# A routed feed-forward layer on one core: router logits taken from the residual itself, and the normalised rows made on POOL during the search

## The reference

```python
h = _layernorm(x) * (1 + ca) + sa
x = x + ga * attn(h)          # linear attention, then an MLP, each through a layer norm
h = _layernorm(x) * (1 + cb) + sb
x = x + gb * ffn(h)

def ffn(h):                   # E = 8, cap = T // E
    logits = h @ Wg
    probs = softmax(logits, axis=-1)
    top_idx = top_k(probs.T, cap)          # each expert takes its cap best tokens
    tok2exp = the best expert of those that chose the token, else its best expert
    out = gate * (gelu(h @ W1[e]) @ W2[e]) for e = tok2exp
```

## Time and profile before

| | us |
|---|---|
| median of 3 runs | 280.67 |
| the three runs | 280.67, 277.25, 280.97 |
| span of the profiled execution | 278.9 |

### The profile page before, as it was taken

The page is one execution under the profiler, slowest core; times in us unless marked ns, Lnnn a source line. Parts: engine busy times, 40 slices in busy tenths (PEclk is TensorE's granted clock), DMA queues, the critical chain, the costliest instruction groups (busy, mean ns, idle before and its releaser), DMA issues.

```text
span 278.9 us, 4426 instructions
## 1 busy us (share of the span) xinstructions
PE 187.5 (67%) x1151; PEld 145.3 (52%) x1151; DVE 178.5 (64%) x668; ACT 123.8 (44%) x394; POOL 129.5 (46%) x207
## 2 busy tenths in 40 slices
PE   0788989796997788486658989550024995865730
PEld 0545759575776658472524475450014975864620
DVE  2679979999977665989898789600001993532330
ACT  2159964474697765448767443110011441232210
POOL 8737303143555444515991002777750045555652
PEclk9999999999799979757675899976555997999975
DMA  5890000001000000000665000633430324433300
GB/s 157 240 328 30 2 1 0 2 0 39 2 0 1 2 1 0 0 2 25 202 182 158 0 2 5 185 98 109 122 106 19 111 72 145 138 117 99 117 34 28
DMA packets 22009, 20.09 MB, mean 72 GB/s; under 512 B 2464, under 2 KB 19360, under 8 KB 21984
## 3 DMA queue, kind: packets, MB, share of 16 engines
q1 hardware_dynamic: 18752, 14.03, 16.9%
q0 software_dynamic: 2240, 5.51, 6.4%
q10 hardware_dynamic: 992, 0.27, 0.8%
HBM read 13.51 MB, written 6.29 MB: 71 GB/s over the span
## 4 chain that ended last, share of the span: by engine, by line
DVE 36%; PE 29%; another core or an unknown queue 14%; POOL 9%; issue 6%; ACT 4%; POOLq 1%; DVEq 0%
PE pH L940 7%; PE pQ L949 6%; DVE x_sb L1133 6%; DVE scr L1274 5%; DVE bn L988 3%; POOL yr L277 3%; DVE t L1085 2%; POOL rs L277 2%; PE pQ L655 2%; DVE x_sb L1086 2%; DVE rows L996 2%; PE pQ L850 1%; DVE t L1084 1%; DVE mv L991 1%
## 5 line engine op out<-in xcount | busy, mean ns | idle before, releaser
L404 POOL DMA_INDIRECT out_dram<-rows,gidx x28 | 28.4, 1014 | 38.2 <-DVE rows L1422 32.6
L401 POOL DMA_INDIRECT rows<-table_dram,gidx x28 | 27.3, 973 | 32.7 <-DVE gidx L1366 24.5
L940 PE MATMUL pH<-x_sb,hid 128*128 (+1 forms) x140 | 25.2, 309 | 20.3 <-issue 19.8
L949 PE MATMUL pQ<-ew,u 128*128 (+1 forms) x140 | 24.7, 303 | 18.6 <-DVE dig L1446 8.8
L621 ACT ACTIVATE u<-pH 128x256 f32<-128x256 f32 x35 | 13.3, 385 | 45.4 <-PE pH L940 30.1
L940 PEld LDWEIGHTS pH<-x_sb,hid 128*128 128x128 f32 x140 | 21.0, 215 | 21.8 <-issue 21.7
L949 PEld LDWEIGHTS pQ<-ew,u 128*128 128x128 f32 x140 | 20.3, 208 | 21.4 <-issue 12.1
L1414 DVE SCALAR_TENSOR_TENSOR t<-pQ,wslot,scr 128x128 f32<-128x128 f32 x35 | 12.1, 347 | 28.0 <-PE pQ L949 18.8
L1398 DVE COPY inv<-pL 128x105 f32<-128x105 f32 x1 | 0.3, 270 | 33.2 <-remote 33.2
L351 POOL TENSOR_TENSOR scr<-feat,z 128x512 f32<-128x512 f32 x8 | 9.6, 1202 | 23.0 <-DVE z L1112 23.0
L762 PE MATMUL pH<-qT,mall 128*128 128x512 f32 x32 | 18.0, 694 | 0.0
(11 more groups left out here) (316 smaller groups left out, 527.6 us busy)
## 6 DMA issues: line engine op xcount, KB each, us to landing
hid<-in_L_ffn_W_dram SPq DMA_DIRECT2D x35, 128.0 KB
table_dram<-x_sb SPq DMA_DIRECT2D x9, 256.0 KB, 2.8
x_sb<-in_L_attn_x_dram SPq DMA_DIRECT2D x8, 256.0 KB, 6.9
table_dram<-rows SPq DMA_DIRECT2D x7, 256.0 KB, 2.3
ew<-in_L_ffn_W_dram SPq DMA_DIRECT2D x2, 512.0 KB, 7.5
w1d<-in_L_ffn_W_dram SPq DMA_DIRECT2D x1, 1024.0 KB, 9.9
rows<-table_dram,gidx POOLq DMA_INDIRECT x28
out_dram<-rows,gidx POOLq DMA_INDIRECT x28
```

The source lines that it names most:

```text
L401: gp.indirect_dma_start(row[:, t, :], None, table[:, :], bass.IndirectOffsetOnAxis(gidx[:, t:t + 1], 0)).then_inc(gathered[t], 16)
L404: gp.indirect_dma_start(out.rearrange("b l d -> (b l) d"), bass.IndirectOffsetOnAxis(gidx[:, t:t + 1], 0), row[:, t, D:2 * D], None).then_ ...
L940: mm = te.matmul(pH[i % 2][:, f * P:(f + 1) * P], wcur[:, i % RW, f * P:(f + 1) * P], xt[:, bass.ds(i - e, 1), :], start=True, stop=True)
L949: mm = te.matmul(pQ[i % 2][:, 0:D], eh[:, i % 2, f * P:(f + 1) * P], ew[:, bass.ds(e, 1), f * D:(f + 1) * D], start=(f == 0), stop=(f == 1))
```

## The change

Five things are done, which hang together.

- **The logits come from the residual.** PE transposes `x_sb` itself as soon as the group is updated, ACT only copies the result, and the matrix is `wgc`: `wg` scaled by `1 + cb`, with each column's mean taken off, so that the token's mean drops out. The norm's scale `rs` and a constant row `cR` (from `sb`) are applied in the softmax: `v_soft_max` first multiplies by `rs`, then adds `cR`. `wgs`, `wgc` and `cR` are made in stage 1 by three small products on PE and four small DVE instructions.
- **The steps are shorter by one**, and POOL's `rs3(s-5)` trails by one more step. The last group is no longer halved.
- **The normalised rows of seven groups** are made by POOL in `h2tok`, four instructions of 128x128 a group. ACT and PE make the last group's for the dense part, now behind the softmax's exponentials (`a_xn3_last`, `p_tx_dense`, `a_h2_last`).
- **The softmax's parts** are 28 and 4 tiles; the gate's rows (`prep_gb`) are made behind it, and the keys in one piece (`v_keys`).
- **The dense part starts later**: `d_gelu(0)` moves from ahead of the search's first round to behind its counts.

```diff
@@ stage 1: the router's matrix and constant @@
+                    te.wait_ge(S["prep_done"], 1)
+                    te.wait_ge(S["wgs_done"], 1)
+                    te.matmul(pH1[:, 400:400 + B * E], ones[:, :], wgs[:, :, :].rearrange("p b e -> p (b e)"), start=True, stop=True)
+                    for b in range(B):
+                        mm = te.matmul(pH1[:, 416 + b * E:416 + (b + 1) * E], colm[:, 2, b:b + 1].to_broadcast([P, P]), wg[:, :],
+                                       start=True, stop=True)
+                    mm.then_inc(S["cm_ready"], 1)
...
+            def centre_router():
+                dve.wait_ge(S["cm_ready"], 1)
+                dve.wait_ge(S["wgs_done"], 1)
+                dve.scalar_tensor_tensor(wgc[:, :, :].rearrange("p b e -> p (b e)"), pH1[:, 400:400 + B * E], -1.0 / D,
+                                         wgs[:, :, :].rearrange("p b e -> p (b e)"), ALU.mult, ALU.add)
+                dve.tensor_copy(cR[:, :, :].rearrange("p b e -> p (b e)"), pH1[:, 416:416 + B * E]).then_inc(S["wgc_done"], 1)
@@ POOL @@
             def h2tok(g):
-                gp.wait_ge(S["xn3"], g + 1)
+                for t in range(GT):
+                    last = gp.tensor_scalar(xn[:, g, t, :], x_sb[:, g * GT + t, :], mv[:, g, t, 0:1], rs[:, g, t:t + 1],
+                                            ALU.subtract, ALU.mult)
+                link(last)
...
-            for s in range(G + 6):
+            for s in range(G + 5):
                 if s < G:
                     qprime(s)
-                if s == G + 2:
-                    yrs(G - 1)
-                if s == G + 1:
-                    yrs(G - 2)
-                if 0 <= s - 4 < G - 1:
-                    rs3(s - 4)
-                if s - 4 == G - 1:
-                    rs3_half(0)
-                    rs3_half(1)
-                if 0 <= s - 3 < G - 2:
+                if 0 <= s - 5 < G:
+                    rs3(s - 5)
+                if 0 <= s - 3 < G:
                     yrs(s - 3)
@@ ACT @@
-            d_gelu(0)
-            between = {0: (d_gelu, 1), 1: (d_gelu, 2), 3: (d_copy, 0), 4: (d_gelu, 3), 5: (d_gelu, 4), 7: (d_copy, 1), 8: (d_gelu, 5),
+            between = {0: (d_gelu, 0), 1: (d_gelu, 1), 2: (d_gelu, 2), 3: (d_copy, 0), 4: (d_gelu, 3), 5: (d_gelu, 4), 7: (d_copy, 1), 8: (d_gelu, 5),
@@ PE @@
             def p_tx3(g):
-                te.wait_ge(S["xn3"], g + 1)
+                te.wait_ge(S["x1_done"], g + 1)
...
-                    mm = te.transpose(pT[:, t * P:(t + 1) * P], xn[:, g, t, :], ident[:, :])
+                    mm = te.transpose(pT[:, t * P:(t + 1) * P], x_sb[:, g * GT + t, :], ident[:, :])
...
+            def p_tx_dense():
+                te.wait_ge(S["xn3_last"], 1)
+                for t in range(GT):
+                    mm = te.transpose(pF[:, t * P:(t + 1) * P], xn[:, DG, t, :], ident[:, :])
+                mm.then_inc(S["txd"], 1)
...
-                if s == G + 4:
-                    p_lg(G - 3)
-                if 0 <= s - 6 < G:
-                    p_tx3(s - 6)
                 if 0 <= s - 2 < G:
                     p_y1(s - 2)
+                if 0 <= s - 5 < G and s < G + 2:
+                    p_lg(s - 5)
                 if 0 <= s - 3 < G:
                     p_y2(s - 3)
-                if 0 <= s - 7 < G - 3:
-                    p_lg(s - 7)
...
+                if 0 <= s - 5 < G and s >= G + 2:
+                    p_lg(s - 5)
+                if 0 <= s - 4 < G:
+                    p_tx3(s - 4)
@@ DVE: the softmax's first half @@
-                dve.wait_ge(S["lg_ready"], (G - 2, G)[part])
+                dve.wait_ge(S["lg_ready"], (G - 1, G)[part])
+                dve.wait_ge(S["rs3"], (G - 1, G)[part])
+                dve.wait_ge(S["wgc_done"], 1)
+                src = (pL[:, 0:t1 * E], pQ1[:, 0:GT * E])[part]
+                link(dve.tensor_tensor(lgs[:, t0:t1, :], src.rearrange("p (t e) -> p t e", e=E),
+                                       rst[:, t0:t1].unsqueeze(2).to_broadcast([P, t1 - t0, E]), ALU.mult))
+                for b, ts in SOFT[part]:
+                    v = lgs[:, b * TB + ts.start:b * TB + ts.stop, :]
+                    last = dve.tensor_tensor(v, v, cR[:, b, :].unsqueeze(1).to_broadcast([P, ts.stop - ts.start, E]), ALU.add)
```

More of the change, by code:

```diff
@@ L210, in bgroup, with lg_out @@
             return t[:, g * GT:(g + 1) * GT, :]
+        def lg_out(g):
+            return pQ1[:, 0:GT * E] if g == G - 1 else pL[:, g * GT * E:(g + 1) * GT * E]
         def up_bank(k):
@@ L516, in a_h2, with a_xn3_last, a_h2_last @@
                     act.wait_ge(S["lg_ready"], g - 1)
-                act.activation(h2T[:, g % 2, :], pT[:, :], ACT.Identity, bias=colm[:, 2, b:b + 1],
-                               scale=colm[:, 3, b:b + 1]).then_inc(S["h2_done"], 1)
-            def a_xn3(g):
-                act.wait_ge(S["nm_done"], g + 1)
-                if g == 0:
-                    act.wait_ge(S["gt_done"], G)
-                for t in range(GT if g < G - 1 else 2):
+                act.copy(h2T[:, g % 2, :], pT[:, :]).then_inc(S["h2_done"], 1)
+            def a_xn3_last():
+                g = G - 1
+                act.wait_ge(S["nm_done"], 1)
+                for t in range(GT):
                     last = act.activation(xn[:, g, t, :], x_sb[:, g * GT + t, :], ACT.Identity, bias=nm[:, g, t:t + 1],
                                           scale=rs[:, g, t:t + 1])
-                last.then_inc(S["xn3"], 1)
-            def a_h2_first():
-                act.wait_ge(S["tx3"], G)
-                act.wait_ge(S["lg_ready"], G - 2)
-                act.activation(h2T[:, (G - 1) % 2, 0:2 * P], pF[:, 0:2 * P], ACT.Identity, bias=colm[:, 2, B - 1:B],
-                               scale=colm[:, 3, B - 1:B]).then_inc(S["h2_done"], 1)
-            for s in range(G + 6):
-                if s == G + 4:
-                    a_xn3(G - 1)
-                if 0 <= s - 6 < G - 1:
-                    a_h2(s - 6)
+                last.then_inc(S["xn3_last"], 1)
+            def a_h2_last():
+                act.wait_ge(S["txd"], 1)
+                act.wait_ge(S["lg_ready"], G)
+                act.activation(h2T[:, DG % 2, :], pF[:, :], ACT.Identity, bias=colm[:, 2, B - 1:B],
+                               scale=colm[:, 3, B - 1:B]).then_inc(S["h2_last"], 1)
+            for s in range(G + 5):
+                if 0 <= s - 5 < G:
+                    a_h2(s - 5)
                 if 0 <= s - 1 < G:
                     a_qT(s - 1)
-                if s == G + 2:
-                    a_square(G - 1, 1, "y2_ready", "sq2")
-                if 0 <= s - 5 < G - 1:
-                    a_xn3(s - 5)
                 if s == 2:
@@ L562, in _ @@
             a_soft(0)
-            a_h2_first()
             a_soft(1)
+            a_xn3_last()
+            a_h2_last()
             def d_gelu(k):
@@ L760, in p_y1 @@
                     te.wait_ge(S["relu0"], g)
+                else:
+                    te.wait_ge(S["wgc_done"], 1)
                 for f in range(2):
@@ L870, in _ @@
             p_prt(1)
+            p_tx_dense()
+            d_up(0)
             d_up(1)
@@ L1038, in weight_sums @@
                     dve.tensor_scalar(saB[:, b, :], ones[:, :], colm[:, 0, b:b + 1], None, ALU.mult)
+                for b in range(B):
+                    last = dve.tensor_scalar(wgs[:, b, :], wg[:, :], colm[:, 3, b:b + 1], None, ALU.mult)
+                last.then_inc(S["wgs_done"], 1)
                 dve.reduce_sum(rowm[:, 0:1], wm[:, :], AX.X)
@@ L1253, in be_ @@
                 return t[:, :, :].unsqueeze(3).to_broadcast([P, B, E, TB])
+            v_soft_max(0)
+            v_soft_max(1)
+            v_bias_last()
+            v_soft_sum(0)
+            v_soft_sum(1)
             prep_gb()
@@ L1263, in _ @@
             bits = pT[:, 0:B * P].bitcast(I32)
-            v_key(1).then_inc(S["keys"], 1)
+            v_keys().then_inc(S["keys"], 1)
             dve.wait_ge(S["keys"], 1)
```

119 lines of the change are left out of this document (28 added, 91 removed).

## The result

The changed kernel took 280.65 us (median of 20 runs, 279.13 to 282.02), the kernel before beside it 279.45 (20 runs, 277.25 to 280.97): a ratio of 1.0062, 95% interval 1.0041 to 1.0084. It is slower by 1.2 us by the medians and by 1.7 us by the ratio, where a time of 277.8 us was forecast. The profiled execution after has a span of 278.6 us and a time of 280.37.

What follows compares the result with a forecast made beforehand. The prediction took a DVE-POOL loop of 7.87 us a group to bound the second pass; -5.8 + 0.6 + 0.4 + 1.5 + 0.4 = -2.9 us turned 280.67 into 277.8 us, range 273.8 to 284.0.

Steps and rivals of the forecast that it cites:

- The loop and PE as the next bound: Second pass: the DVE-POOL loop of 7.87 us a group goes, and PE bounds it at 7.1.
- The rival of a new wait at PE's transposes: Second pass: router's transposes wait for the update, period returns towards 7.9 us; 281.8 us in all, chance 0.13.
- Gain 5.8 us: Second pass: the last update ends at 113.0 us where the last piece ended at 118.85.
- The way to the keys: From the last update to the search's start: 10.0 us for 9.4, a cost of 0.6.
- Stage 1: The matrix made in stage 1, by small products on PE and DVE instructions, costs 0.4 us.
- The search: First two rounds: 6.8 us for 5.3 with the table load between ACT's counts, a cost of 1.5.
- With 0.33 it is 29.1 us: POOL behind the keys: 28 added 128x128 instructions at 0.33 us; rows take 29.1 us, search 27.6, overlap about nil.
- The forecast's own sign of being wrong: POOL's rows: the forecast is wrong if those 128x128 instructions take more than 0.5 us.
- the forecast's own formula: POOL's rows: with t us an instruction, POOL ends 19.9 + 28t behind the keys; the slots' chain starts at 29.6.
- the term of 0.4 us for POOL's rows: Beyond the overlap, POOL's rows hold up a DVE instruction with two SBUF inputs, by up to 0.8 us; 0.4 taken.
- POOL's rows run into the slots: Rival, slots: at 0.8 us an instruction, 12.7 us overlap costs 6.3, 283.7 us; chance 0.13 for 3 us or more.
- The gathers' wait moves with them: Behind the first gather: DVE's wait of 33.2 us moves with the gathers, unchanged.

Runs made afterwards that it cites:

- the second trace: The kernel before, unchanged, run again on the second chip: 249.36 us against 248.91, ratio 0.9998.
- run 4: The changed kernel with a GELU of 128x1 ahead of ACT's last copy, so that the table load comes early: 280.38 us, ratio 1.0066 to the kernel before.
- run 1: The changed kernel without POOL's 28 instructions that normalise the rows: 277.33 us, ratio 0.9945 to the kernel before.
- run 10: The kernel before with the 28 row instructions added on POOL ahead of each group's product: 282.37 us, ratio 1.0109.
- run 2: The changed kernel with the rows of groups 0 to 5 made on ACT, only group 6's on POOL: 276.43 us, ratio 0.9901 to the kernel before.
- the swap alone: The kernel before with only POOL's order changed, `yr` of the next group ahead of `rs`: 285.49 us, ratio 1.0256.
- run 6: The changed kernel with POOL's old order put back, `rs` ahead of `yr` of the next group: 258.23 us on the second chip, ratio 1.0362 to the kernel before.
- run 7: The changed kernel with POOL's rows of groups 0 to 2 made ahead of the wait for the keys: 250.16 us, ratio 1.0037 to the kernel before.
- run 9: The changed kernel again, 280.83 us, ratio 1.0046 to the kernel before, and the changed kernel with rows on ACT again, 276.74 us, ratio 0.9882.

## Why the prediction was wrong

**The loop and PE as the next bound: right.** The forecast had 7.1 us a group, and it is 7.0. The last update was due at 113.4 (with stage 1) and ended at 113.85. Putting the loop back cost 5.9 us in the pass. The rival of a new wait at PE's transposes did not come: PE is busy for 94% of the 40 us from 60 to 100.

**"Gain 5.8 us": nearly right against one long execution.** The end of 118.85 held 1.35 us of a lower clock in one product of that execution, which the second trace does not have. Against its own trace the pass gained 5.35 us, against the second one 3.9. The 280.67 us were the median of the three runs shown, and are the second highest of the twenty, whose median is 279.45. The time forecast doesn't hang on this, since the changed kernel's pass was worked out by itself; the gain does: 277.8 us is 2.9 below 280.67 and only 1.65 below 279.45.

**The way to the keys: right**, 9.57 for 10.0. Stage 1 cost 0.6 us for 0.4: from DVE's first product on the features to group 1's update it is 54.3 us for 53.7. Most of it stands between the products of groups 5 and 6, 2.80 us apart for 2.18.

**The search: the sum right, the parts not.** The second round ended 1.4 us later, counted from the start of the search, for 1.5. But I had the table load as the cause and the dense products within its time; run 4 shows that the products make 1.1 of it, in the first round. And the whole search lost only 0.8, since `klo` now had no POOL product beside it.

**"With 0.33 it is 29.1 us": the step that failed.** The instruction takes 0.80 us, 2.4 times the select of the same size; that its two scalar operands by pointer, which the select has not, are the reason isn't shown. The bounds, 0.25 and 0.55, didn't hold it, and the 0.19 us estimated among the rivals is a quarter of it. The forecast's own sign of being wrong, more than 0.5 us for one, came. By the forecast's own formula POOL's end comes 42 us behind the keys (41.0 measured) and the overlap is 12.7 (13.6 measured, 150.8 to 164.4). So the term of 0.4 us for POOL's rows is the one that was mis-sized: the slots took 2.9 to 3.5 us more. The rival "POOL's rows run into the slots", at 0.13, is what happened. Its price for such an overlap, 6.3 us, was too high. It took all of POOL's instructions to hold DVE up, where only the products of two tensors do, 2.6 of each group's 5.8 us. Run 1 shows the size in the changed kernel (2.6 us in the slots), run 10 in the one before (5.9 us, with all of the slots beside POOL's work). This step alone turned the sign: without the rows the kernel is faster than before (ratio 0.9945, run 1), and with them on ACT as well (0.9901, run 2).

**The gathers' wait moves with them: right**, 41.16 us from `gidx` to `inv` for 41.19.

Term by term against the trace that the forecast was made from, forecast first: ahead of group 1's update +0.4 and +0.35; the pass -5.8 and -5.35; to the keys +0.6 and +0.2; the search +1.5 and +0.8; the slots +0.4 and +3.1; to `inv` 0 and 0; the last stretch 0 and +0.7. The sums are -2.9 and -0.3 us, and the slots' 2.7 us are the whole of the miss in the span; the other misses cancel, which is luck.

The sum by stretches against the second trace of before, with 0.6 for stage 1: +0.6 - 3.9 + 0.2 + 0.7 + 2.9 to 3.3 = +0.5 to +0.9 us. The timed ratios say +1.3 to +1.7, with intervals down to 0.4. What is left, 0.5 to 1 us, is of the size by which the last stretch differs between executions (66.5 and 67.5 us for the changed kernel), and isn't told apart from that.

## What to carry to other kernels

Price a new instruction by a row of its own kind; where there is none, take the range wide enough that what it decides can fall either way, and ask for each place that the engine's work is pushed to, which instruction of the neighbour it will meet. Before a gain is taken from the chain of one execution, look in it for a row whose duration differs from its siblings in the other steps: it may be missing in the next execution. And when an order on one engine is the bound, list who else waits, in program order, for the step that is put back; the swap alone made this kernel slower by 2.6%.

## What the runs showed of the hardware

**POOL holds DVE up by instruction.** In the changed kernel's search and slots, DVE's long rows all lie beside POOL's two-tensor products; beside its 128x128 instructions with one tensor the same kinds keep their time within 0.14 us (`klo` 0.48, `m` 0.56 for 0.42), and POOL's own rise from 0.79 to as much as 0.87 there. A row that is held up ends a fixed time behind the end of POOL's product: its own undisturbed duration less 0.12 to 0.15 us, in the four rows shown above and in 22 more of five traces (those of runs 4, 6, 7, 9 and 10; `klo` has no undisturbed row to go by; `rank` of run 10 ends at 162.21, 0.54 behind 161.67, with 0.69 as its own duration). So what a product costs can be read off two rows: the part of it that is left when DVE's instruction starts, less some 0.14 us. Among those held up are a cast and a `tensor_scalar` of 128x32, with one tensor each (1.22 and 0.61 for 0.18). The Trainium skill (SBUF — State Buffer, Who interferes with whom) names these two among the instructions that can take the shared pair of ports; the trace agrees for both. It also says that whoever comes second is blocked for the whole of the other's instruction; that holds for POOL's products but for those 0.14 us, and not for its one-tensor instructions.

**The wait of 33 us goes with the chip.** From `gidx` to `inv` it is 41.2 to 41.3 us in the ten traces from other chips, and 11.2 to 11.4 in the four of the second chip. There the kernel before, unchanged, with the same gathers from 169.69 us on, has `inv` at 179.79 instead of 40 us behind the first gather, and then works on the experts while POOL issues the other gathers. The profile's page of that trace:

```profile
L401 POOL DMA_INDIRECT rows<-table_dram,gidx x28 | 28.4, 1013 | 32.9 <-DVE gidx L1366 24.7
```

and DVE's timeline there:

```profile
179.79 0.27 DVE L1398 COPY inv<-pL 128x105 f32<-128x105 f32 x1 [3.16 <-PE pL L958]
```

In the first trace of before PE's last product for `inv` had ended by 187.0 us (PE's timeline), the last of POOL's gathers by 207.4, and DVE went on at 212.04.

```profile
185.94 1.06 PE L958 MATMUL pL<-featT 128*128 128x105 bf16 x14
```

What holds it up there isn't shown by any run here. In every other stretch of the table the two traces of the kernel before agree within 1.5 us, which is why runs from both chips can stand in it.
